# Tridiagonalization step: the norm read from the matrix product, two broadcast passes for its sums, one gate on both reciprocals

## What is computed

```python
deg = jnp.sum(A, axis=0) + jnp.sum(A, axis=1) - jnp.diagonal(A)
L = jnp.diag(deg) - A
L_norm = d_inv_sqrt[:, None] * L * d_inv_sqrt[None, :]
_, U = jnp.linalg.eigh(L_norm)
agg = jnp.einsum('mn,bnd->bmd', U.T, features)
```

## Time and profile before

| | us |
|---|---|
| runs of the kernel before | 6158.05, 6162.72, 6484.39 (median 6162.72) |
| the profiled execution | 6150.05, its span 6147.9 |
| the 510 steps, from 888 to 3605 in the span | 2717 |
| all that follows them | 2543 |

### The profile page before, as it was taken

How to read it: one execution, slowest core, us unless ns; L and a number is a source line. 1 busy time by engine, 2 the same in 40 slices (tenths; PEclk the granted TensorE clock), 3 DMA queues, 4 the chain that set the end, 5 groups by cost and what they waited for, 6 DMA issues and landing times.

```text
span 6147.9 us, 78861 instructions
## 1 busy us (share of the span) xinstructions
PE 3290.3 (54%) x19000; PEld 2342.0 (38%) x19000; DVE 4304.7 (70%) x27212; ACT 932.4 (15%) x4314; POOL 790.6 (13%) x3424
## 2 busy tenths in 40 slices
PE   7877738888888888777777730000002212230476
PEld 4333226565566666666666630000002212120243
DVE  1222286666677777888888889999968888889534
ACT  2432201111122222222222210000000000000000
POOL 0000001111111111111100014444430000000000
PEclk9988855555555555555555555555555555565578
DMA  2000000000000000000000000000000000000000
GB/s 55 0 0 0 0 0 1 1 1 1 1 1 1 1 1 1 1 1 1 1 1 1 1 1 1 1 1 1 1 1 0 0 0 0 0 0 0 0 0 27
DMA packets 20805, 17.38 MB, mean 3 GB/s; under 512 B 6544, under 2 KB 16784, under 8 KB 20368
## 3 DMA queue, kind: packets, MB, share of 16 engines
q1 hardware_dynamic: 20368, 12.65, 0.8%
HBM read 8.41 MB, written 4.20 MB: 2 GB/s over the span
## 4 chain that ended last, share of the span: by engine, by line
DVE 53%; PE 37%; issue 6%; ACT 2%; SPq 1%; POOL 0%; DMA 0%; DVEq 0%; ACTq 0%; POOLq 0%
PE bank L487 9%; PE bank L436 5%; PE bank L499 5%; PE bank L491 3%; DVE qp L1193 2%; PE bank L470 2%; PE bank L438 2%; DVE ycol L934 2%; DVE dif L1546 2%; PE bank L482 2%; DVE ts L966 1%; DVE qp L1183 1%; DVE tau_row L950 1%; DVE jcol L958 1%; DVE gated L948 1%
## 5 line engine op out<-in xcount | busy, mean ns | idle before, releaser
L487 PE MATMUL bank<-lapw,hid 128*32 128x160 f32 (+3 forms) x10200 | 660.3, 421 | 61.2 <-DVE lapw L907 17.8
L524 PE MATMUL bank<-diag,blk 128*128 128x32 f32 (+1 forms) x96 | 23.3, 416 | 1041.4 <-DVE diag L1310 1030.0
L487 PEld LDWEIGHTS bank<-lapw,hid 128*32 128x32 f32 x10200 | 395.1, 163 | 190.7 <-DVE lapw L969 83.0
L499 PE MATMUL bank<-xp,ones 128*128 128x1 f32 x1020 | 298.9, 362 | 277.9 <-DVE xp L958 277.9
L524 PEld LDWEIGHTS bank<-diag,blk 128*128 128x128 f32 x96 | 21.4, 327 | 1043.5 <-DVE diag L1310 1031.9
L219 POOL TENSOR_TENSOR sq<-hid,ltm 128x4 f32<-128x4 f32 (+3 forms) x510 | 101.0, 198 | 2324.3 <-DVE hid L961 2265.7
L497 PE MATMUL bank<-xp,ones 128*128 128x1 f32 x1020 | 299.0, 362 | 185.4 <-DVE xp L940 185.4
L436 PE MATMUL bank<-hid,onehot 128*128 x504 | 328.2, 769 | 120.0 <-DVE ga L736 67.2
L499 PEld LDWEIGHTS bank<-xp,ones 128*128 128x128 f32 x1020 | 255.3, 311 | 321.6 <-DVE xp L958 321.6
L497 PEld LDWEIGHTS bank<-xp,ones 128*128 128x128 f32 x1020 | 255.3, 311 | 229.1 <-DVE xp L940 229.1
L470 PE MATMUL bank<-xn,ones 128*128 128x2 f32 x1020 | 299.3, 363 | 18.5 <-DVE xn L887 17.6
(11 more groups left out here) (729 smaller groups left out, 8493.1 us busy)
## 6 DMA issues: line engine op xcount, KB each, us to landing
out_x<-xs SPq DMA_DIRECT2D x16, 256.0 KB, 3.3
lapw<-in_adj SPq DMA_DIRECT2D x1, 1024.0 KB, 5.9
bias_rows<-in_L_gnn_bg SPq DMA_DIRECT2D x8, 64.0 KB, 5.6
hid<-lz SPq DMA_DIRECT2D x32, 1.0 KB, 1.7
bias_rows<-in_L_gnn_b SPq DMA_DIRECT2D x4, 64.0 KB, 5.7
wg<-in_L_gnn_Wg SPq DMA_DIRECT2D x2, 64.0 KB, 11.0
wg<-in_L_gnn_W SPq DMA_DIRECT2D x2, 64.0 KB, 3.6
xs<-in_x SPq DMA_DIRECT2D x1, 0.5 KB, 19.7
```

Source lines behind the costliest of these rows:

```text
L487: m = pe.matmul(bank[1][32 * q:32 * q + 32, 0:(T + 1) * 32].rearrange("p (u i) -> p u i", i=32), acols[:, t, k:k + 1].to_broadcast([P, 32] ...
L499: pe.matmul(bank[2][:, 4 * NB:4 * NB + 1], ones[:, 0:P], xp[:, 1:2], start=True, stop=True).then_inc(vp_ps, 1)
```

## The change

The Householder vector v is no longer made. The masked column a itself (`am`) goes into the panel in its place, and GpSimd writes it there. A unit column is put into the panel slot that will later hold w. The product of a with these two columns gives the leading entry of a and the sum of squares of the rest, and VectorE picks both out of the product (`al`). ScalarE takes the root of them, GpSimd two coefficients (`coef`), and VectorE makes from these the two weights (`wts`) and the two reciprocals, which one instruction gates together (`gt`). Of the broadcast sums two are left, of two and of three columns. GpSimd's sums for the gate are gone; it now writes the panel columns, the coefficients and the masked columns `yam`. The rows that used to be kept at each step on VectorE are written by ScalarE. After the loop the diagonals are put together from other rows, with about twelve more vector instructions.

In the diff, lines removed on GpSimd, ScalarE and VectorE are left out (they stand above).

```diff
 
...
             for k in range(STEPS):
...
+                t0, j = (k + 1) // P, k % NB
+                T = NT - t0
+                if k == 0:
+                    pool.wait_ge(a_ready, 1)
+                else:
+                    pool.wait_ge(y_done, k)
+                if j == 0 and k:
+                    pool.wait_ge(panx_ps, k // NB)
+                pool.tensor_copy(pan[:, t0:, :, j, 0], onehot[:, t0:, k + 1].unsqueeze(2).to_broadcast([P, T, 4])).then_inc(am_ready, 1)
                 pool.wait_ge(a_ready, k + 1)
...
+                pool.tensor_tensor(pan[:, t0:, :, j, 1], acols[:, t0:, k].unsqueeze(2).to_broadcast([P, T, 4]),
+                                   ltm[:, t0:, k + 1].unsqueeze(2).to_broadcast([P, T, 4]), ALU.mult).then_inc(am_ready, 1)
+                pool.wait_ge(al_ready, k + 1)
+                pool.tensor_scalar(coef[:, 1:2], al[:, 0:1], al[:, 0:1], al[:, 1:2], ALU.mult, ALU.add).then_inc(coef_ready, 1)
+                pool.tensor_scalar(coef[:, 0:1], al[:, 0:1], 0.0, 0.5, ALU.is_ge, ALU.subtract).then_inc(coef_ready, 1)
+                pool.wait_ge(a1_ready, k + 1)
+                pool.tensor_tensor(xd[:, 0:1], ya[:, t0, 0:1], ident[:, (k + 1) % P:(k + 1) % P + 1], ALU.mult).then_inc(x2_ready, 1)
+                pool.tensor_tensor(yam[:, t0:, :], ya[:, t0:, :], ltm[:, t0:, k + 1].unsqueeze(2).to_broadcast([P, T, 2]), ALU.mult).then_inc(a1_masked, 1)
             pool.memset(spare[:, 1:2], 0.0).then_inc(rot_used, 1)
             pool.memset(spare[:, 2:3], 0.0).then_inc(rot_used, 1)
             for w in range(SWEEPS):
...
                 t0, j = (k + 1) // P, k % NB
...
                 if j == 0 and k:
                     act.wait_ge(panx_ps, k // NB)
                     act.activation(panx[:, 0, t0 * P:], bank[1][0:2 * NB, t0 * P:], ACT.Copy)
                     act.activation(panx[:, 1, t0 * P:], bank[2][0:2 * NB, t0 * P:], ACT.Copy).then_inc(panx_sb, 1)
                     act.wait_ge(updated, k // NB)
+                if k == 0:
+                    act.wait_ge(a_ready, 1)
                 act.activation(tz[:, t0:, 0], lap[:, t0:, k + 1], ACT.Copy).then_inc(edge_ready, 1)
...
+                act.wait_ge(am_ready, 2 * k + 2)
+                act.activation(swap[:, t0:, j, 0], pan[:, t0:, 0, j, 1], ACT.Copy).then_inc(v2_ready, 1)
+                act.wait_ge(al_ready, k + 1)
+                act.activation(root[:], al[:, 0:1], ACT.Sqrt, scale=al[:, 0:1], bias=al[:, 1:2]).then_inc(norm_root, 1)
+                act.wait_ge(g_ready, k + 1)
                 act.wait_ge(p_ready, k + 1)
...
+                act.activation(w0[:, t0:], pcol[:, t0:], ACT.Copy, scale=gt[:, 0:1]).then_inc(w0_ready, 1)
+                act.activation(wts[:, 2:3], gt[:, 1:2], ACT.Copy).then_inc(g_copied, 1)
+                act.activation(gt_row[:, k, :], gt[:, 0:2], ACT.Copy)
+                act.activation(p_row[:, k:k + 1], wts[:, 1:2], ACT.Copy)
+                act.wait_ge(w_ready, k + 1)
+                act.activation(swap[:, t0:, j, 1], pan[:, t0:, 0, j, 0], ACT.Copy).then_inc(w2_ready, 1)
+                act.activation(ends_row[:, k, :], bank[0][:, 0:2], ACT.Copy).then_inc(vy_saved, 1)
             act.activation(tz[:, NT - 1:, 0], lap[:, NT - 1:, N - 1], ACT.Copy).then_inc(edge_ready, 1)
 
             for w in range(SWEEPS):
...
                 T, c0 = NT - t0, t0 * P
-                pe.wait_ge(norm_in, 2 * (k + 1))
-                pe.matmul(bank[0][:, 0:2], ones[:, 0:P], xn[:, 0:2], start=True, stop=True).then_inc(norm_ps, 1)
                 if k:
                     pe.wait_ge(w_ready, k)
-                    pe.wait_ge(v2_ready, k)
                 if j == 0 and k:
                     pe.wait_ge(w2_ready, k)
+                    pe.wait_ge(v2_ready, k)
                     for t in range(t0, NT):
                         pe.transpose(bank[1][0:2 * NB, t * P:(t + 1) * P], lapw[:, t, N:N + 2 * NB], ident[:])
                         m = pe.transpose(bank[2][0:2 * NB, t * P:(t + 1) * P], swap[:, t, :, :].rearrange("p j s -> p (j s)"), ident[:])
@@ -481,6 +479,8 @@
                     for t in range(t0, NT):
                         pe.matmul(bank[4 + t][:, c0:], panx[:, 0, t * P:(t + 1) * P], panx[:, 1, c0:], start=True, stop=True).then_inc(update_ps, 1)
                     pe.wait_ge(updated, k // NB)
+                pe.wait_ge(a_ready, k + 1)
+                pe.wait_ge(am_ready, 2 * k + 2)
                 for t in range(t0, NT):
                     strips = lapw[:, t, c0:].rearrange("p (u q i) -> p u q i", q=4, i=32)
                     for q in range(4):
@@ -491,15 +491,12 @@
                     pe.matmul(bank[2][:, 0:2 * j], unit(k), lapw[:, t0, N:N + 2 * j], start=True, stop=True).then_inc(rowz_ps, 1)
                 if k:
                     pe.wait_ge(vy_saved, k)
-                pe.wait_ge(tail_in, k + 1)
-                pe.matmul(bank[4][:, 0:1], ones[:, 0:P], xn[:, 2:3], start=True, stop=True).then_inc(tail_ps, 1)
-                pe.wait_ge(x_ready, k + 1)
-                pe.matmul(bank[3][:, 0:1], ones[:, 0:P], xp[:, 0:1], start=True, stop=True).then_inc(vy_ps, 1)
+                pe.wait_ge(x_ready, 2 * k + 2)
+                pe.matmul(bank[3][:, 0:2], ones[:, 0:P], xd[:, 1:3], start=True, stop=True).then_inc(vy_ps, 1)
                 pe.wait_ge(x2_ready, k + 1)
-                pe.matmul(bank[2][:, 4 * NB:4 * NB + 1], ones[:, 0:P], xp[:, 1:2], start=True, stop=True).then_inc(vp_ps, 1)
+                pe.matmul(bank[0][:, 0:3], ones[:, 0:P], xd[:], start=True, stop=True).then_inc(vy2_ps, 1)
             j = STEPS % NB
             pe.wait_ge(w_ready, STEPS)
-            pe.wait_ge(v2_ready, STEPS)
             pe.matmul(bank[2][:, 0:2 * j], unit(STEPS), lapw[:, NT - 1, N:N + 2 * j], start=True, stop=True).then_inc(rowz_ps, 1)
             pe.wait_ge(diag_in, 1)
             for t in range(NT):
...
                 dve.wait_ge(y_done, k + 1)
+                V.tensor_scalar(al[:], bank[1][:, here:here + 2], 1e-36, None, ALU.add).then_inc(al_ready, 1)
                 a = put(V.tensor_tensor(yz[:, t0:, 0:32], bank[1][:, 0:T * 32].rearrange("p (t i) -> p t i", i=32),
                                         pick[:].unsqueeze(1).to_broadcast([P, T, 32]), ALU.mult))
                 if j:
                     dve.wait_ge(w2_ready, k)
...
                     a = put(V.tensor_tensor(yz[:, t0:, 32:32 + 2 * j], panel_cols(j, t0), panel_rows(bank[1][:, T * 32:T * 32 + 32], j, T), ALU.mult))
+                after(a)
+                y = put(V.tensor_reduce(ya[:, t0:, 1], yz[:, t0:, 0:32 + 2 * j], AX.X, ALU.add))
+                dve.wait_ge(edge_ready, k + 1)
+                if j:
                     rowz += 1
                     dve.wait_ge(rowz_ps, rowz)
                     c = put(V.tensor_tensor(tz[:, t0:, 1:1 + 2 * j], panel_cols(j, t0), panel_rows(bank[2], j, T), ALU.mult))
...
+                after(y)
+                V.tensor_tensor(xd[:, 2:3], ya[:, t0, 1:2], ident[:, e:e + 1], ALU.mult).then_inc(x_ready, 1)
+                V.tensor_tensor_reduce(jcol[:, 0, t0:], a_, ya[:, t0:, 1], 1.0, 0.0, ALU.mult, ALU.add, xd[:, 1:2]).then_inc(x_ready, 1)
                 if j:
                     after(c)
...
+                V.tensor_reduce(ya[:, t0:, 0], tz[:, t0:, 0:1 + 2 * j], AX.X, ALU.add).then_inc(a1_ready, 1)
+                dve.wait_ge(norm_root, k + 1)
+                r = put(V.reciprocal(ts[:, 0:1], root[:]))
+                dve.wait_ge(coef_ready, 2 * k + 2)
+                after(r)
+                r = put(V.tensor_scalar(ts[:, 1:2], ts[:, 0:1], coef[:, 1:2], root[:], ALU.mult, ALU.add))
+                after(r)
+                p = put(V.tensor_tensor(wts[:, 1:2], ts[:, 1:2], coef[:, 0:1], ALU.mult))
+                after(p)
+                q = put(V.tensor_scalar(wts[:, 0:1], al[:, 0:1], wts[:, 1:2], coef[:, 1:2], ALU.mult, ALU.add))
+                dve.wait_ge(a1_masked, k + 1)
                 if k:
                     dve.wait_ge(w0_ready, k)
...
+                V.scalar_tensor_tensor(pcol[:, t0:], yam[:, t0:, 0], wts[:, 1:2], yam[:, t0:, 1], ALU.mult, ALU.add).then_inc(p_ready, 1)
+                after(q)
+                q = put(V.reciprocal(inv[:], wts[:, 0:2]))
+                after(q)
+                V.scalar_tensor_tensor(gt[:, 0:2], al[:, 1:2].to_broadcast([P, 2]), 1e-24, inv[:], ALU.is_gt, ALU.mult).then_inc(g_ready, 1)
                 dve.wait_ge(p_ready, k + 1)
...
+                dve.wait_ge(g_ready, k + 1)
+                b = put(V.scalar_tensor_tensor(nbcol[:, t0:], pcol[:, t0:], gt[:, 1:2], yam[:, t0:, 0], ALU.mult, ALU.subtract))
                 dve.wait_ge(vy_ps, k + 1)
...
+                z = put(V.tensor_tensor_reduce(jcol[:, 1, 0:2], bank[3][:, 0:2], gt[:, 1:3], 1.0, 0.0, ALU.mult, ALU.add, zy[:, 0:1]))
+                h = put(V.tensor_scalar(turnf[:], gt[:, 0:1], gt[:, 0:1], wts[:, 1:2], ALU.mult, ALU.mult))
+                after(z)
```

(23 more changed lines are left out.)

132 lines of the change are left out of this document (26 added, 106 removed).

## The result

| | us |
|---|---|
| runs of the changed kernel | 6306.02 to 6316.28 (median 6312.04, 4 runs) |
| runs of the kernel before, beside it | median 6161.5 (4 runs) |
| ratio | 1.0246 (95% interval 1.0225 to 1.0266) |
| span of the profiled execution | 6311.4 (before 6147.9) |

The changed kernel is slower by 150 us. The forecast was 6303 us, the range 6225 to 6400. One of the four runs of the kernel before (6484.39 us) was a slow one; the ratio leaves it out.

The account below looks back on a forecast made before the run. Bound: a closed chain across engines, repeated 510 times. Steps without update 135 us, with update 14 (149 in all), after the loop 4: +153 on 6150 gives 6303 us, range 6225 to 6400.

Parts of the forecast that it names:

- The rules for starts: Start delays read from the old trace: VectorE independent 0.08 before the predecessor's end, dependent 0.03 after it, read-out at 0.08.
- the walk: Instruction-by-instruction timing of one changed step from the product's start; T = 4, j = 8: 6.06 becomes 6.48 us, +0.42.
- The second wait: At L921 and L936: 0.07 us more is lost where the wait ending last is the second of two.
- the rival without it: Waits cost nothing extra: L921 and L936 each start 0.07 earlier, 71 us less, 6232 us; chance 0.28.
- The front at T = 1: Start of T = 1 steps: reading the product at 0.51 gains 0.60, all paid back later; step +0.02 us.
- 0.18 is exposed: Steps with T = 2: L924 starts 1.12 after the product's start where 0.94 would do; 0.18 subtracted, growth +0.31.
- The steps with an update: 31 steps without the panel part's cover: growth about 0.52 for T = 4 to 2, 0.2 for T = 1; 14 us.
- After the loop: About twelve more vector instructions on the path behind the loop: 3 to 7 us, taken as 4.
- Two roads to the product: Next product's start at T = 4: by w, or by GpSimd writing a into the panel; both end at 6.48.
- cover: Time by which another engine's result is there before VectorE reads it; thinnest 0.14 (gate's copy) and 0.24 (masked columns).
- GpSimd beside VectorE: Rival: GpSimd's six operations a step hold VectorE up, 0.19 a step, 97 us more, 6400 us; chance 0.15.
- The clock: Rival: TensorE's clock granted at the upper level through the loop, 330 us less, 5973 us; 0.05 with any other gain.

Follow-up runs that it names:

- The swap: Changed kernel with the two waits ahead of L921 and of L936 written in the other order, last-ending one first: 6250.2 us, ratio 1.0139.

## Why the prediction was right

**What bounds the kernel** was read rightly: a closed chain across engines. TensorE's 583 us and VectorE's 280 us of saved work bought nothing, since neither stood on the part of the chain that grew.

**The rules for starts** carried the sum. Independent 0.08 ahead of the end, dependent 0.03 behind it, the read-out at 0.08: over some twenty instructions the walk ends at 6.10 where it was to end at 6.18. Of these 0.08, 0.06 are there by L913 (3.41 instead of 3.47), the rest comes behind L939.

**The second wait** was the boldest step: one instruction (L886) and one of TensorE stood behind it, and the rival without it had 0.28. The swap confirmed it with 0.08 at both places, and the lone records show what it consists of.

**The front at T = 1** came out right for a reason stated wrongly. "A reader at 0.51 would have gained 0.60" is true of the product's reader alone; the panel row's reader could gain only 0.26, as the kernel without the norm shows. The walk had this row in it (L910 at 1.09, measured 1.09), and therefore the sum held. At T = 2 "0.18 is exposed" is the step that failed: without the norm nothing is gained there. As bookkeeping it did no harm: the reader of the product does start 0.20 sooner (0.93 instead of 1.13), what follows it is 0.45 longer (0.49 in the forecast), and w's lead on the product grows by 0.05. At j = 8 the growth is 4.69 - 4.40 = 0.29, against 0.31.

**The steps with an update** grew by 0.38, 0.49, 0.49 and 0.18 for T = 4 to 1, 12 us in all against 14. **After the loop** 5.1 against 4.

**What was missing** is the gap. The steps without an update in which it tells in neither kernel grow by 0.39, 0.34, 0.29 and 0.01 for T = 4 to 1, which is 122 us over all of them, against 140.5 measured and 135 forecast. So the gap is worth about 19 of the 152.5 us, and the walk was about 13 us too dear in the ordinary steps (0.03, 0.04, 0.02 and 0.01 a step) and 2 in those with an update. That the loop comes within 4 us of the forecast's 149 is therefore luck in part: two misses of opposite sign. Most of the other 6 us between 6303 and 6312 lie ahead of the first w.

**Two roads to the product** were to end together, 0.30 behind w. They do not: by the lone waits of TensorE the panel column's road decides in the steps without an update, and the product starts 0.35 behind w. GpSimd is through at 6.30 of the walk, where 6.37 was forecast, but from there to the product it is 0.15 and not 0.11. The 0.11 had been read from a weight load (L477); the product's weight load does start 0.11 behind the panel column, its first matmul 0.03 later. By w alone, at 6.10, the product could have started at 6.40, so this road costs about 0.05 a step, an estimate of 25 us. The sum did not show it, since both roads ran ahead of the walk: the end is at 6.45 and not 6.48. ScalarE's root takes 0.39 and not 0.30, but is there at 3.01 of the walk and read at 3.63: its cover held, as did that of `coef`.

**The rivals.** GpSimd beside VectorE costs nothing (6311.15 us with ten of its operations a step instead of six). The clock is granted at 0.50 over the whole loop, the lower of its levels, with TensorE now only 55% busy; so that rival fell by the window row alone.

## What to carry over

Saving work of a busy engine does not pay when the step is a chain across engines: what counts is on which side of the awaited product an instruction stands, and here the norm moved from the free side to the paid side. The same instructions in another order were worth 194 us, 62 of them by the order of two pairs of waits alone, so after moving work onto the path, interleave dependent small instructions with independent ones before judging the idea. Among an instruction's waits put the one that ends last first, and look for the lone waits in the trace to see which one that is.

## What the runs showed of the hardware

- The wait written first stays with its instruction; those behind it become lone records ahead of it (21 ns with one wait on VectorE, 50 to 51 ns with two, and 51 on TensorE with one or two). One that ends last in such a record costs 0.07 to 0.08 us more on VectorE (L921, L936); on TensorE the product starts 0.15 behind what ended last instead of 0.05.
- VectorE pauses with nothing to wait for once in 128 of its records, lone waits included: every 4.00 steps in the changed kernel (32 records a step), every 3.75 with 34. Where the pause tells, a step is 0.1 to 0.37 us longer.
- Four GpSimd operations of 8 columns, 0.68 us in one piece, did not lengthen VectorE's instructions beside them, which read and wrote SBUF as well.
